# Attention and ffn on one core: the tail's order of work, its drain, and when the first batch's parts are made again

## The reference, cut to what matters

```
q, k, v = x @ Wq.T, x @ Wk.T, x @ Wv.T          (16 heads of 64)
scores  = (q * min(cond, 4)) @ k.T / 8, causal mask, softmax
y       = (softmax @ v) @ Wo.T
scale   = max(max|y| of the row, 1e-5) / 127    y_q = clip(round(y / scale), -128, 127)
alpha   = max(mean|W|, 1e-5)                    w_q = clip(round(W / alpha), -1, 1)
out     = x + (y_q * scale) @ (w_q * alpha).T + bias
```

## Time and profile before

| | us |
|---|---|
| median of 3 runs | 2014.2 (2012.69 to 2015.3) |
| profiled execution, device time | 2013.14 |
| its span, first to last instruction | 2011.2 |
| PE busy | 1928.2 (96%) |
| DVE busy | 1321.4 (66%) |
| ACT busy | 1028.7 (51%) |
| POOL busy | 918.1 (46%) |
| mean granted TensorE clock | 0.993 of full |

### The profile page before, as it was taken

The page is one execution under the profiler, slowest core; times in us unless marked ns, Lnnn a source line. Parts: engine busy times, 40 slices in busy tenths (PEclk is TensorE's granted clock), DMA queues, the critical chain, the costliest instruction groups (busy, mean ns, idle before and its releaser), DMA issues. The chain is left out here.

```text
span 2011.2 us, 39534 instructions
## 1 busy us (share of the span) xinstructions
PE 1928.2 (96%) x12378; PEld 1687.6 (84%) x12378; DVE 1321.4 (66%) x3330; ACT 1028.7 (51%) x2495; POOL 918.1 (46%) x985
## 2 busy tenths in 40 slices
PE   8899999999999999999999999999978999999996
PEld 6788787899998999998999989999866777777772
DVE  6354455577788777788777787777774744434433
ACT  4333333577777777777777777777762000000000
POOL 1343443444466444466444574444454343443433
PEclk9999999999999999999999999999989999999999
DMA  6799998978788787877878778787824233333323
GB/s 211 287 340 328 338 346 320 353 231 298 249 282 297 243 291 253 278 284 268 291 248 280 262 276 281 242 299 244 258 90 162 63 95 94 106 114 95 115 84 146
DMA packets 163269, 469.74 MB, mean 234 GB/s; under 512 B 12496, under 2 KB 84176, under 8 KB 133456
## 3 DMA queue, kind: packets, MB, share of 16 engines
q1 hardware_dynamic: 162624, 467.72, 67.3%
q10 hardware_dynamic: 528, 0.52, 0.1%
HBM read 325.59 MB, written 109.05 MB: 216 GB/s over the span
## 5 line engine op out<-in xcount | busy, mean ns | idle before, releaser
L218 PE MATMUL proj_ps<-parts 128*128 128x256 f32 x5376 | 765.6, 290 | 9.4 <-DMA parts<-x_scratch 3.3
L218 PEld LDWEIGHTS proj_ps<-parts 128*128 128x128 f32 x5376 | 674.1, 190 | 20.1 <-DVE k_sum L253 4.4
L336 POOL TENSOR_TENSOR prob<-prob,row_inv 128x128 f32<-128x128 f32 (+3 forms) x512 | 379.4, 741 | 555.7 <-DVE row_inv L330 555.1
L324 ACT ACTIVATE prob<-prob,row_min 128x128 f32<-128x128 f32 (+3 forms) x512 | 287.6, 562 | 138.6 <-DVE row_min L318 132.2
L370 DVE TENSOR_TENSOR pt_all<-t_ps,pt_all 128x128 fp32r<-128x128 f32 (+3 forms) x512 | 249.3, 487 | 57.0 <-ACT pt_all L363 55.6
L318 DVE CUSTOM_DVE_ANT_0 prob<-s_ps,mask 128x128 f32<-128x128 f32 (+3 forms) x512 | 248.3, 485 | 27.3 <-issue 3.9
L346 PE MATMUL t_ps<-ident,prob 128*128 128x128 f32 x1280 | 227.5, 276 | 26.3 <-DVE pt_all L370 19.1
L662 ACT ACTIVATE yt_q<-t_ps 128x1024 bf16<-128x1024 bf16 x32 | 32.7, 1023 | 399.6 <-PE t_ps L655 399.6
L363 ACT ACTIVATE pt_all<-t_ps 128x128 fp32r<-128x128 f32 (+3 forms) x512 | 217.0, 424 | 4.6 <-PE t_ps L346 2.2
L346 PEld LDWEIGHTS t_ps<-ident,prob 128*128 128x128 f32 x1280 | 152.1, 141 | 51.2 <-issue 25.1
L608 PE MATMUL proj_ps<-wo_parts,o_parts 128*128 128x512 f32 x768 | 190.3, 403 | 0.0
(11 more groups left out here) (138 smaller groups left out, 2761.1 us busy)
## 6 DMA issues: line engine op xcount, KB each, us to landing
parts<-x_scratch SPq DMA_DIRECT2D x224, 1024.0 KB, 9.9
x_scratch<-xv SPq DMA_DIRECT2D x112, 512.0 KB, 4.5
k_sw<-k_st SPq DMA_DIRECT2D x128, 256.0 KB, 3.8
v_scratch<-v_tmp SPq DMA_DIRECT2D x64, 256.0 KB, 3.9
v_raw<-v_scratch SPq DMA_DIRECT2D x32, 512.0 KB, 3.9
oT_scratch<-o_sum SPq DMA_DIRECT2D x64, 256.0 KB, 2.8
o_raw<-oT_scratch SPq DMA_DIRECT2D x32, 512.0 KB, 4.9
x_tile<-x SPq DMA_DIRECT2D x32, 512.0 KB, 4.3
```

The lines of the kernel that those rows point to most:

```text
L218: mm = pe.matmul(qk_bank(w, m), wc[w][:, c, wp, k, :], xq[:, c, :, xp, k, :], start=(fresh and k == 0 and i == 0), stop=(k == CH - 1 and i ...
L324: act.activation(prob[u % QT], prob[u % QT], ACT.Exp, bias=row_min[:, u % 4:u % 4 + 1], scale=-1.0, accum_out=row_sum[:, u % 4:u % 4 + 1]) ...
L336: pool.tensor_tensor(prob[u % QT], prob[u % QT], row_inv[:, u % 4:u % 4 + 1].broadcast_to([P, w]), ALU.mult).then_inc(norm_done, 1)
```

## The change

In the value stage, part 0 of FIRST is made again beside pair 4 rather than 3, parts 1 and 2 both beside pair 5 rather than at 4 and 5, and POOL's sums for it move to pairs 5 and 6. In the tail: for t < 8 the transposes of t - 1 come behind both halves of Wo of tile t; the weights' sum comes behind the second half of tile 2; `wf_scale` comes behind `quantise` of tile 2; the ternary weights are made at t = 3 to 6; POOL makes x + bias of tiles 0 and 1 at t = 4 and 5. In the drain the products 25, 27, 29, 31 go to the banks `y_ps[0]` (`proj_ps`), which Wo has left, each product waits for the finish of the one two before it, and the transposes of tile 31 stand behind product 25. The last tile's halves are finished and stored each by itself.

```diff
--- before.py
+++ after.py
@@ -527,6 +527,8 @@
         y_done = sem("y_done")
         q_chain = sem("q_chain")
         f_scale_done = sem("f_scale_done")
+        f_half_done = sem("f_half_done")
+        res_half_done = sem("res_half_done")
         y_free = sem("y_free")
         yq_done = sem("yq_done")
         yt_done = sem("yt_done")
@@ -662,20 +664,31 @@
             act.activation(yt_q[:, t % LAG, :, :].rearrange("p k q -> p (k q)"), yt_ps, ACT.Copy)\
                .then_inc(ytq_done, 1)
 
+
+        DRAIN = TILES - LAG
+
+        def f_out(t, half):
+            return (y_ps[0] if t > DRAIN and (t - DRAIN) % 2 == 1 else f_ps)[half][:, :]
+
         def ternary(pe, t, p):
             pe.wait_ge(ytq_done, t + 1)
             if isinstance(t, int) and t == 0:
                 for parity in range(2):
                     pe.wait_ge(o_sum_done[parity], STEPS * NBLK + 1)
                 pe.wait_ge(wf_q_done, KT)
+            elif t <= DRAIN:
+                pe.wait_ge(res_done, t)
+            elif t == DRAIN + 1:
+                pe.wait_ge(y_free, TILES - 1)
             else:
-                if due(count := t):
-                    pe.wait_ge(res_done, count)
+                pe.wait_ge(res_done, t - 1)
             for half in range(2):
                 w = slice(half * HALF, (half + 1) * HALF)
                 for k in range(KT):
-                    mm = pe.matmul(f_ps[half][:, :], yt_q[:, t % LAG, k, :], wf_q[:, k, w],
+                    mm = pe.matmul(f_out(t, half), yt_q[:, t % LAG, k, :], wf_q[:, k, w],
                                    start=(k == 0), stop=(k == KT - 1))
+                if t == TILES - 1 and half == 0:
+                    mm.then_inc(f_half_done, 1)
             mm.then_inc(f_done, 1)
 
         def load_tile(sp, t, p):
@@ -699,18 +712,35 @@
             dve.tensor_scalar(f_scale[:, p:p + 1], y_scale[:, t:t + 1], alpha[:, 0:1], None, ALU.mult)\
                .then_inc(f_scale_done, 1)
             dve.wait_ge(f_scale_done, t + 1)
-            dve.wait_ge(f_done, t + 1)
+            if t < TILES - 1:
+                dve.wait_ge(f_done, t + 1)
             dve.wait_ge(x_bias_done, t + 1)
             if due(count := (t - p) * 8 + 1):
                 dve.wait_ge(out_done[p], count)
             for half in range(2):
                 w = slice(half * HALF, (half + 1) * HALF)
-                r = dve.scalar_tensor_tensor(out=res[:, p, w], in0=f_ps[half][:, :],
+                if t == TILES - 1:
+                    if half == 0:
+                        dve.wait_ge(f_half_done, 1)
+                    else:
+                        dve.wait_ge(f_done, TILES)
+                r = dve.scalar_tensor_tensor(out=res[:, p, w], in0=f_out(t, half),
                                              scalar=f_scale[:, p:p + 1], in1=x_bias[:, p, w],
                                              op0=ALU.mult, op1=ALU.add)
+                if t == TILES - 1 and half == 0:
+                    r.then_inc(res_half_done, 1)
             r.then_inc(res_done, 1)
 
         def store(sp, t, p):
+            if t == TILES - 1:
+                for half in range(2):
+                    w = slice(half * HALF, (half + 1) * HALF)
+                    if half == 0:
+                        sp.wait_ge(res_half_done, 1)
+                    else:
+                        sp.wait_ge(res_done, TILES)
+                    sp.dma_start(out[bass.ds(t * P, P), w], res[:, p, w]).then_inc(out_done[p], 16)
+                return
             sp.wait_ge(res_done, t + 1)
             sp.dma_start(out[bass.ds(t * P, P), :], res[:, p, :]).then_inc(out_done[p], 16)
 
@@ -733,7 +763,7 @@
 
 
         FIRST, SECOND = (0, True), (1, True)
-        AGAIN = {3: (FIRST, (0,)), 4: (FIRST, (1,)), 5: (FIRST, (2,)), 6: (FIRST, (3,)), 7: (FIRST, (4,)),
+        AGAIN = {4: (FIRST, (0,)), 5: (FIRST, (1, 2)), 6: (FIRST, (3,)), 7: (FIRST, (4,)),
                  8: (FIRST, (5, 6)), 10: (SECOND, (0,)), 11: (SECOND, (1,)), 12: (SECOND, (2,)),
                  13: (SECOND, (3, 4)), 14: (SECOND, (5, 6))}
 
@@ -772,8 +802,8 @@
         def sums_in(n):
 
             made = []
-            for e, (a, b, c) in ((FIRST, (4, 5, 6)), (SECOND, (11, 12, 13))):
-                made += [(e, k) for k in {a: (1, 2), b: (3,), c: (4,)}.get(n, ())]
+            for e, at in ((FIRST, {5: (1, 2), 6: (3, 4)}), (SECOND, {11: (1, 2), 12: (3,), 13: (4,)})):
+                made += [(e, k) for k in at.get(n, ())]
             if n + 1 < PAIRS:
                 made += [((n + 1, False), k) for k in (1, 2, 3, 4)]
             return made
@@ -1081,7 +1111,7 @@
                 .then_inc(v_ur_done, 1)
 
 
-        WF_AT = {2: (0,), 3: (1,), 4: (2, 3), 5: (4,), 6: (5, 6), 7: (7,)}
+        WF_AT = {3: (0, 1), 4: (2, 3), 5: (4, 5), 6: (6, 7)}
 
         def load_wf(sp, k):
             if k == 0:
@@ -1791,7 +1821,7 @@
                     store(sp, f - 1, (f - 1) % 2)
             store(sp, TILES - 1, 1)
             for p in range(2):
-                sp.wait_ge(out_done[p], TILES // 2 * 16 + 1)
+                sp.wait_ge(out_done[p], (TILES // 2 + p) * 16 + 1)
 
         @block.tensor
         def _(pe):
@@ -1805,15 +1835,19 @@
                 attention_out(pe, 1, 1, 1, k)
             for t in range(2, TILES):
                 attention_out_half(pe, t, t % 2, 0)
-                transpose_y(pe, t - 1, (t - 1) % 2)
+                if t >= LAG:
+                    transpose_y(pe, t - 1, (t - 1) % 2)
+                attention_out_half(pe, t, t % 2, 1)
+                if t < LAG:
+                    transpose_y(pe, t - 1, (t - 1) % 2)
                 if t == 2:
                     wf_add_partitions(pe)
-                attention_out_half(pe, t, t % 2, 1)
                 if t >= LAG:
                     ternary(pe, t - LAG, t % 2)
-            transpose_y(pe, TILES - 1, 1)
             for t in range(TILES - LAG, TILES):
                 ternary(pe, t, t % 2)
+                if t == DRAIN + 1:
+                    transpose_y(pe, TILES - 1, 1)
 
         @block.scalar
         def _(act):
@@ -1834,9 +1868,10 @@
             dve.wait_ge(const_ready, CONSTS)
             program(dve, dve_step)
             quantise(dve, 1, 1)
-            wf_scale(dve)
             for t in range(2, TILES):
                 quantise(dve, t, t % 2)
+                if t == 2:
+                    wf_scale(dve)
                 for k in WF_AT.get(t, ()):
                     wf_ternary(dve, k)
                 if t >= LAG:
@@ -1860,11 +1895,11 @@
                                base=0, pattern=[[-1, P]], channel_multiplier=1).then_inc(fills, 1)
             v_pool(pool)
             program(pool, pool_step)
-            add_bias(pool, 0, 0)
-            add_bias(pool, 1, 1)
             for t in range(2, TILES + LAG):
                 if t + 1 < TILES:
                     split_o(pool, t + 1, (t + 1) % 2)
+                if t in (4, 5):
+                    add_bias(pool, t - 4, t % 2)
                 if 0 <= t - LAG < TILES - 2:
                     add_bias(pool, t - LAG + 2, t % 2)
```

## The result

The changed kernel takes **1994.74 us** (median of 4 runs, 1992.99 to 1995.15), the kernel before 2014.02 beside it: a ratio of 0.9911 (95% interval 0.9899 to 0.9923), 18 us or 0.9% faster. The forecast was 1994.5. The profiled execution took 1994.49 us with a span of 1992.7, against 2013.14 and 2011.2, so its own time fell by 18.65 us, where the sum said 19.7.

The account below looks back on a forecast made before the run. PE, busy for 96% of the span, was taken as the bound, so only its idle and low-clock stretches could be won. 5.9 + 0.7 + 12.2 + 0.9 = 19.7 us off 2014.2 gave 1994.5, range 1991 to 1998.5.

Parts of the forecast that it names:

- Part 1: Value stage, first batch's parts made again later: shorter gap in pair 3 and kept clock gain 5.9 us, bounds 0.8 and 5.9.
- I take it that the clock stays up: Value stage, behind pair 3's shortened gap: PE keeps its high clock, which gives back 2.95 us.
- rival 1: The clock falls in a short gap, pair 3's or the one before product 24: price 2.9 us, 1997.4; chance 0.17.
- I take 0: Value stage, pair 4: no stall for stores like pair 10's, cost 0; other end 1.03 us a pair.
- Part 2: The tail's start, reordered work around tiles 2 to 8: gain 0.7 us, bounds -1.4 and 3.6.
- 1.55 for the gap's end: Tail, tile 3: PE starts it 1.55 us earlier, at 1543.5, after 8.1 us of idleness.
- The 2.05 for five waits of 0.41: Tail, tiles 4 to 8: PE's five waits of 0.41 us for DVE's y_q go, gaining 2.05 us.
- at t = 8 tile 7's y_q is asked for 0.43 us later than before, just enough: Tail, where the old order returns: tile 7's y_q is ready in time, so PE has no wait there.
- x + bias at nothing: Tail, t = 4 and 5: POOL's moved sums, 4.69 us, fit its 7.2 us free per tile and cost nothing.
- Part 3: The drain: ffn products start every 3.45 us rather than 5.27, gaining 12.2 us.
- the 3 us in hand: The drain: the first chain of finish, POOL's sum and load of x has 3 us more to spare.
- Part 4: The last tile, finished and stored in halves: gain 0.9 us, bounds 0.7 and 2.

Follow-up runs that it names:

- the second profile: The changed kernel run again without an edit, on another chip: 1996.78 us, ratio 0.9911 to the kernel before.

## Why the prediction was right

**Part 1** was right in its mechanism and ordering: pair 4's load is late next, landing after 8.0 us (8.2 forecast), and the gap is 2.25 us (2.54). The stage's 5.6 us against 5.9 are partly luck: 0.75 of them were there before the gap opened, ahead of anything that was changed. Two terms were off. The first, "I take it that the clock stays up", worth 2.95, held at the place and failed for the kernel. In the profiled execution attention's first 84 matmuls behind a 2.79 us gap took 12.96 us rather than 10.34, which the kernel before doesn't pay. In other executions pair 3 itself pays. The earlier trace rows had shown one 2.8 us gap with full clock; one sample of a gap doesn't show that such gaps are safe. This was rival 1, at 0.17; its price of 2.9 lies between what the traces show (some 1.6 us a place in the second profile; in the first, from attention's first product to the first scores, 33.92 us rather than the kernel before's 29.37), its chance was far too low: it came true in all eleven profiles. In the profiled pair of traces the loss shows as only 0.5 us over all of attention, and that is luck. Counted from attention's first product, PE is still 2.9 us behind the kernel before some 80 us later (78.71 us rather than 75.77 to the same product of the scores at 405.66 and 408.31), although it waited less for transfers by then (1.2 us rather than 3.3). It makes this up in the last 450 us, and the length of attention scatters by up to 5.9 us from profile to profile. The second is the stall that pair 10 had, for which "I take 0" stood. It came: 0.63 us of wait and 1.1 us in all. The landing times of the earlier trace rows were those of a pair that PE had reached late; with the gap gone the same bytes come closer together and land in 7 us. In the changed kernel's second profile, where low clock held pair 3 up, ACT waited 3.82 us for that store rather than 5.72 and pair 5 had no wait.

**Part 2.** 1.55 for the gap's end was 1.7; 8.1 us of idleness was 8.20. The low clock behind it cost 2.26, not 2.9: the granted clock was 0.50 already from 1533.4 to 1538.2, while PE had nothing to do, and that part cost nothing. The 2.05 for five waits of 0.41 was 2.8, as tiles came 0.56 us closer (11.44, not 12.00). Two steps failed. The first is "at t = 8 tile 7's y_q is asked for 0.43 us later than before, just enough": its age was taken from a DVE that is free when a product ends. The second is x + bias at nothing. I had counted POOL's time and not what runs beside it: the two sums stretched DVE's y_q at tiles 3 and 4 by 2.1 us each, and with two slices a tile, put at nothing as well, DVE had no time left to make that up. PE then waited 2.20 us, 2.3 with its restart. The runs show that both are needed: with the sums back in front (same slices, same 11.44 us a tile) the wait is gone, and with one slice less it is gone too. The sum for part 2, 0.7, stands against -0.1 in the traces, and nothing in the runs.

**Part 3** was exact in the profiled pair: 3.45 us a product, 12.2 in all, the clock at 1.00, x never late for PE. The loads of x landed in up to 5.2 us, more than the 4.5 that I had said cost nothing; the 3 us in hand took that up. What I hadn't named is the wait that came: DVE for a store of two tiles before, since I priced the loads' landing and not the stores'. At 5.4 us it used up DVE's slack and none of PE's. The gap before product 24, which rival 1 names too, did cost the clock in four of the eleven profiles that have it: the next product then came 5.1 us behind it rather than 3.45. The Trainium skill's section "A second HAM failure mode: psum-queue depth-cycling" in "TensorE: Matmul & The Clock Gate", cited against this part, isn't borne out for products that follow each other without a gap: 1.00 over eight of them. That a clock which falls and rises again between bursts costs throughput, as it says, fits what the gaps at pair 3 and at attention's start did; there it was waits for DVE, and not a change of banks, that made the gaps.

**Part 4**: 1.3 for 0.9; the half store landed in 2.0 to 2.3 us rather than 2.6.

The total hit since the misses were small beside the 12.2: 0.3 in the value stage (1.1 at pairs 4 and 5, most of it hidden by the early start of the gap), 0.5 in attention, 0.8 in part 2, with 0.4 made up by the last step.

## What to carry to other kernels

Where a consumer holds the only banks, a second pair that an earlier stage has left can be worth the whole wait, as here, and its price can be read from start-to-start times before it is built. When work is moved into another engine's free time, look at what it will run beside: POOL's two sums fitted in POOL's time, made two instructions of DVE 2.1 us longer each, and PE waited 2.2 us for it some tiles later, since DVE had two slices in every tile and no slack. And look at a load's place in its queue together with the order of the engine that waits for it: with the split first in POOL's order, moving one load of 0.5 MB ahead of 5.5 MB gave 6.4 us, while the reordering without it gave nothing that could be measured.

## What the runs showed of the hardware that I had not expected

Gaps of 2.2 to 2.8 us between dense products can cost TensorE its high clock, in one execution and not in another of the same kernel. Of eleven profiles each, the gap at pair 3 (2.2 to 2.5 us) was followed by low clock in seven, the one at attention's start (2.8) in seven, the one ahead of product 24 (2.45) in four; one of the first two always paid. In the two profiles with a gap of over 5 us in pair 3 the clock fell there and not at attention's start. Why a given gap pays in one execution and not in the next stays open. Matmuls that nobody reads kept the clock up in the gaps that they filled (three places in two profiles), and the work behind them started no later for them. Their worth for a whole kernel is shown for the two short gaps only, and narrowly: 1990.5 to 1993.1 us filled, 1993.0 to 1998.5 unfilled on the same chip.

DVE's instructions that write `y_q` and `wf_q` (128x1024 bf16) took 0.69 or 0.70 us in 502 cases of the fourteen traces' tails and 2.27 to 2.79 us in the other 58; the 58 are exactly those that began while a POOL instruction was running. Moving POOL's two sums away took y_q of tile 3 back to 0.69 us.
